# One Mamba-and-experts layer on one core: corrections and u on GpSimd, a PSUM bank for the convolution, three banks for turned states

## The chip, the cores and the metric

The kernel runs on one core of one Trainium2 chip. The metric is device time in microseconds of one execution, the median of three. The core has five engines that take instructions in order, each from its own queue, and wait for each other through semaphores: TensorE (PE), VectorE (DVE), ScalarE (ACT), GpSimd (POOL) and SyncE (SP), which here only issues DMAs. PSUM has eight banks of 128 x 512 float32 values; all eight are in use before and after the change.

## The reference

```python
x = x + mamba(cond(x, subject))          # the part that the change touches
x = x + ffn(adapters(x))                 # experts, after all blocks

# mamba, cut to its shape: 2048 tokens in rows of 64, 1024 channels, 16 states
xz = hidden @ in_proj.T;  x, z = split(xz)
xc = silu(sum(conv_w[:, k] * x_padded[:, k:k + L] for k in range(4)))
dt, B, C = split(xc @ x_proj.T)
delta = softplus(dt @ dt_proj.T + dt_bias)
h = h * exp(delta * A_n) + (delta * xc) * B_n      # a scan over tokens, for each state n
y = sum_n(h_n * C_n);  y = (y + xc * D) * silu(z);  out = y @ out_proj.T
```

The softplus is made from max(v, 0) + log(1 + e) with e = exp(-|v|). A *correction* makes the logarithm exact: w = 1 + e is rounded, and e - (w - 1) is what rounding lost; it is added to ln(w). The product delta * xc is called u.

## The kernel before

The 2048 tokens are four blocks (`j`) of 512. Channels lie on partitions, 8 groups (`d`) of 128 of them, tokens along the free axis, so that most tiles are 128 x 512. A block has 32 steps (`m`): two halves of 16, one for channel groups 0 to 3, one for 4 to 7, and in each half a step per state `n`. In one step, for four channel groups `i`:

- ScalarE makes `da` = exp(delta * A) in one of two PSUM banks (L823);
- GpSimd makes `dbx` = u * B from a broadcast row `b_all` that SP loads (L1077), one buffer for each `i`;
- VectorE scans, h = h * da + dbx (L965);
- TensorE turns the four token tiles `t` of the state into PSUM (`hT`, L623), since the sum over states needs tokens on partitions to scale by C;
- VectorE adds tiles 0 to 2, scaled by C, to `yacc` (L977, L983). Tile 3 is scaled by ScalarE into `stage` (L838) and added by a DMA that GpSimd issues (L1083), except in the last two states of a half.

VectorE's order in a step is: scans 0 and 1, the sums of tiles 0 and 1 of the step before, scans 2 and 3, the sum of tile 2. The products of step m + 1 may start when the scans of step m are done, group by group. The DMA of a step adds what ScalarE scaled two steps before.

Beside this, the pieces of `BESIDE` fill the engines: projections of this block and of the next. Each entry is a step. Names matter here: `x`e is an input projection with its convolution, `z`e a gate projection, `dt`d and `ln`d the softplus of channel group d, `cond`, `rank`, `bc`, `out`, `w`, `xr`, `row` other projections and transposes, `turn` the turning of `yacc`, `gate` the product with silu(z). TensorE does a step's pieces in that step, one before turning the first tiles and the others between tiles. ScalarE does them one step later, and so do VectorE's corrections and convolutions, behind the last sum of the step; VectorE's u and GpSimd's half of `ln` come two steps later, on GpSimd behind the step's DMA issue. In the first half ln4 to ln7 stand at steps 3, 5, 7 and 9, in the second ln0 to ln3 (for the next block) at 23 to 26. The last block has no pieces for a next block: no `x`, no ln0 to ln3. Ahead of the blocks the pieces of `AHEAD` run alone. SP loads `b_all` and the projections' weights in one queue, in which each weight load waits until the projection that held its slot is done.

A correction and u are VectorE's (`correct`, `make_u`); GpSimd adds the correction to the logarithm and the sum to delta (`finish_delta`, L1050 and L1052). The convolution is a product by ScalarE into `xc` (L679) and three sums by VectorE in place, in SBUF (L880).

Of the kernel before, what the change touches and what calls it, by code (L numbers as in the profile page):

```python
# [21 lines left out]
P = 128  # L22
# [54 lines left out]
BANKS = 2  # L77

# [139 lines left out]
def mamba(nc, ctx, arena, ident, logits, parts, x_pad, itok, cond_w, cond_b, rows_d, in_wT, xp_wT, dt_wT, out_wT, chan, ident_d,  # L218
# [60 lines left out]
    hT = [ps(f"hT{t}", [P, HT * P]) for t in range(TB)]  # L279
# [34 lines left out]
    sp_step = sem("sp_step")  # L314
    sp_ready = sem("sp_ready")
# [24 lines left out]
    x2_rows = x2_d[0:TOK].rearrange("(k t p) f -> k t p f", t=TB, p=P)  # L340

    with nc.Block() as block:
# [99 lines left out]
        def _(pe):  # L442
# [170 lines left out]
            def turn_h(j, m, tiles):  # L613

                pe.wait_ge(scan_done, j * SCANS + SCAN0 + HT * (m + 1))
                last = (j, m - 1) if m else (j - 1, STEPS - 1)
                for t in tiles:
                    if last[0] >= 0 and shifted(last[1], t):
                        pe.wait_ge(scaled[t], scaled_by_act(*last))
                    elif last[0] >= 0:  # L620
                        pe.wait_ge(sum_done, sums_by_dve(*last, t))
                    for d in range(HT):
                        mm = nc.tensor.transpose(hT[t][:, d * P:(d + 1) * P], h[:, m % RING, d, t * P:(t + 1) * P],  # L623
                                                 ident[:])
                    mm.then_inc(hT_full, 1)
# [8 lines left out]
            for j in range(NBLK):  # L634
                for m in range(STEPS):
# [12 lines left out]
        def _(act):  # L648
# [18 lines left out]
            def conv_in(section, at, e):  # L667

                act.wait_ge(bank_full, at.full + 1)
                if section == "ahead":  # L670
                    if e >= RING:
                        act.wait_ge(conv_step, (TAPS - 1) * (e - RING + 1))
                else:
                    act.wait_ge(conv_step, at.block * ((TAPS - 1) * DT) + (TAPS - 1) * (e - RING + 1))
                    act.wait_ge(u_ready, (at.block - 1) * DT + e + 1)
                    act.wait_ge(skip_ready, (at.block - 1) * DT + e + 1 + SKIP0)
# [54 lines left out]
            def log1p(section, at, d):  # L731
# [8 lines left out]
                nc.scalar.activation(sp_w[:, s, :], sp_e[:, s, :], ACT.Identity, bias=1.0)  # L740
                nc.scalar.activation(u[:, d, :], sp_e[:, s, :], ACT.Ln, bias=1.0).then_inc(sp_ready, 1)
# [1385 lines left out]
```

## Time and profile before

| | us |
|---|---|
| median of three runs | 2019.96 (2019.82 to 2022.29) |
| the profiled execution, own time | 2020.74 |
| its span | 2018.9 |
| PE, DVE, ACT, POOL busy in the span | 1700.3, 1498.0, 854.7, 1087.3 |
| the four blocks, first scan to last | 121.3 to 1185.7 |

A busy share over the whole span hides the stages: VectorE is full in the blocks, TensorE behind them. Read idle time together with what ended it, and by stretches. Instructions of one engine overlap by some 0.06 us in the profile, so the distance between two starts is what one costs.

### The profile page before, as it was taken

To read this page: it belongs to the slowest core of one execution; us is meant where nothing else is said; L and a number is where in the kernel's file an instruction comes from. 1 tells how busy PE (TensorE), PEld (TensorE's weight loads), DVE (VectorE), ACT (ScalarE), POOL (GpSimd) and SP (SyncE) were. 2 spreads that over 40 slices of the span, in tenths; PEclk is the share of its full clock that TensorE was granted. 3 is DMA by queue.
4 is the path that set the end of the run, shared out by engine and by line. 5 is a ranking of instruction groups with operands and counts; after the bars stand their busy time and mean duration, and the time that the engine had idled before them with its cause. 6 is when DMAs were issued, how large, how long until landed. Compare 5 with 4: busy or idle time off the path is not lost. (4 is left out here: it accounts for less than half of the span.)

```text
span 2018.9 us, 28413 instructions
## 1 busy us (share of the span) xinstructions
PE 1700.3 (84%) x7908; PEld 1265.4 (63%) x7908; DVE 1498.0 (74%) x1925; ACT 854.7 (42%) x1274; POOL 1087.3 (54%) x871
## 2 busy tenths in 40 slices
PE   3856787698888888887867778989989999999998
PEld 2345444464545554446545554877868999999997
DVE  0379989999999999899999960567725566656564
ACT  0456656466576466665575531100002223323232
POOL 0079569677589596597797963000004344334433
PEclk9968878698898798887988879899999999999999
DMA  4223323344335244234343453211215666666664
GB/s 99 68 60 90 89 58 79 84 101 105 94 85 139 76 106 117 66 87 134 84 111 88 116 162 123 72 63 63 85 34 130 168 153 148 154 151 146 168 159 75
DMA packets 146915, 211.45 MB, mean 105 GB/s; under 512 B 24976, under 2 KB 83104, under 8 KB 143584
## 3 DMA queue, kind: packets, MB, share of 16 engines
q1 hardware_dynamic: 109200, 132.52, 20.7%
q0 software_dynamic: 32832, 72.12, 19.4%
q10 hardware_dynamic: 4720, 4.86, 0.9%
q8 instruction: 76, 1.25, 0.3%
q14 instruction: 87, 0.71, 0.1%
HBM read 277.64 MB, written 38.15 MB: 156 GB/s over the span
## 5 line engine op out<-in xcount | busy, mean ns | idle before, releaser
L1077 POOL TENSOR_TENSOR arena_kept<-arena_kept,b_all 128x512 f32<-128x512 f32 x512 | 671.8, 1422 | 196.5 <-DVE arena_kept L965 167.5
L965 DVE TENSOR_TENSOR_SCAN arena_kept<-da,arena_kept 128x512 f32<-128x512 f32 x512 | 596.5, 1203 | 37.6 <-PE hT L623 16.6
L823 ACT ACTIVATE da<-arena_kept,a_neg 128x504 f32<-128x504 f32 x512 | 346.9, 685 | 333.9 <-DVE arena_kept L965 330.3
L623 PE MATMUL hT<-ident_kept,arena_kept 128*128 128x128 f32 x2048 | 326.3, 318 | 172.7 <-DVE arena_kept L965 167.5
L623 PEld LDWEIGHTS hT<-ident_kept,arena_kept 128*128 128x128 f32 x2048 | 286.1, 166 | 265.9 <-DVE arena_kept L965 216.9
L472 PE MATMUL bank<-hid,wt 128*128 128x512 f32 x512 | 258.0, 653 | 22.8 <-ACT arena_kept L679 22.1
L983 DVE SCALAR_TENSOR_TENSOR yacc<-hT,c_now,yacc 128x512 f32<-128x512 f32 x376 | 263.4, 730 | 9.8 <-PE hT L623 8.8
L1981 POOL DMA_INDIRECT out<-y,slots_kept x76 | 132.7, 1745 | 238.4 <-issue 155.4
L472 PEld LDWEIGHTS bank<-hid,wt 128*128 128x128 f32 x512 | 105.0, 215 | 136.2 <-issue 111.8
L1617 POOL DMA_DIRECT2D slots_kept<-lists_kept x1 | 0.6, 569 | 253.1 <-DVE lists_kept L1567 253.1
L880 DVE SCALAR_TENSOR_TENSOR arena_kept<-xpad,ch,arena_kept 128x512 f32<-128x512 f32 x96 | 87.5, 911 | 63.0 <-ACT arena_kept L679 60.7
L1849 ACT ACTIVATE gs<-egp 128x352 f32<-128x352 f32 x73 | 33.8, 463 | 234.9 <-PE eup L1181 234.4
L533 PE MATMUL bank<-skip,wt 128*128 128x512 f32 x256 | 123.0, 629 | 2.5 <-DVE skip L914 2.5
L1976 POOL DMA_INDIRECT xg_kept<-x_scratch,slots_kept x72 | 74.8, 1038 | 78.7 <-ACT y L1888 42.2
L1083 POOL DMA_DIRECT2D yacc<-stage x104 | 97.3, 935 | 34.1 <-DVE arena_kept L965 21.0
L1929 DVE TENSOR_TENSOR a<-gs,eup 128x352 f32<-128x352 f32 x73 | 37.8, 518 | 92.3 <-ACT gs L1849 92.3
L1050 POOL TENSOR_TENSOR arena_kept<-arena_kept 128x512 f32<-128x512 f32 x32 | 48.8, 1524 | 101.6 <-DVE arena_kept L888 101.6
L1179 PE MATMUL egp<-w_up_hi_kept,xT_hi 128*128 x292 | 101.0, 346 | 2.9 <-DVE w_up_lo_kept L1173 2.9
L1455 ACT ACTIVATE sgs<-gp 128x512 f32<-128x512 f32 x24 | 14.4, 598 | 197.0 <-PE gp L1181 197.0
L1169 DVE CAST aT_hi<-aT_ps 128x256 fp32r<-128x256 f32 (+1 forms) x144 | 44.4, 350 | 68.5 <-PE aT_ps L1806 68.5
L1180 PE MATMUL egp<-w_up_lo_kept,xT_hi 128*128 x292 | 94.9, 325 | 0.0
L1181 PE MATMUL egp<-w_up_hi_kept,xT_lo 128*128 x292 | 94.7, 324 | 0.0
(217 smaller groups left out, 3394.4 us busy)
## 6 DMA issues: line engine op xcount, KB each, us to landing
w_up_kept<-in_up_T SPq DMA_DIRECT2D x76, 1408.0 KB, 6.1
w_dn_kept<-in_dn_T SPq DMA_DIRECT2D x76, 768.0 KB, 7.4
b_all<-bt_scratch SPq DMA_DIRECT2D x128, 256.0 KB, 3.6
yacc<-stage POOLq DMA_DIRECT2D x104, 256.0 KB, 4.5
wt<-in_in_T SPq DMA_DIRECT2D x64, 256.0 KB, 3.0
wt<-in_out_T SPq DMA_DIRECT2D x32, 256.0 KB, 3.0
x_in<-in_x_pad ACTq DMA_DIRECT2D x16, 256.0 KB
res<-in_x_pad SPq DMA_DIRECT2D x16, 256.0 KB, 4.5
```

The lines of the kernel that those rows point to most:

```text
L472: mm = nc.tensor.matmul(bank[:], w[:, k, :], hid[:, at.block % RING, k, :], start=(k == 0), stop=(k == KM - 1))
L533: mm = nc.tensor.matmul(bank[:], w[:, d, :], skip[:, part * HT + d, :], start=(part == 0 and d == 0), stop=False)
L623: mm = nc.tensor.transpose(hT[t][:, d * P:(d + 1) * P], h[:, m % RING, d, t * P:(t + 1) * P], ident[:])
L823: nc.scalar.activation(out[:, :, 1:], rows[:, :, 1:], ACT.Exp, scale=a_neg[:, d, n:n + 1]) \
L965: nc.vector.tensor_tensor_scan(h[:, n % RING, i, :], da[i % RING][:], dbx[:, i, :], 0.0, ALU.mult, ALU.add).then_inc(scan_done, 1)
L983: nc.vector.scalar_tensor_tensor(out=yacc[:, t, :], in0=hT[t][:], scalar=scalar, in1=yacc[:, t, :], op0=ALU.mult, op1=ALU.add).then_inc(su ...
L1077: nc.gpsimd.tensor_tensor(dbx[:, i, :], u[:, d, :], b_all[:, m % RING, :], ALU.mult) \
L1083: nc.gpsimd.dma_start(out=yacc[:, t, :], in_=stage[:, SHIFTED.index(t), :], accum_op=ALU.add) \
L1179: nc.tensor.matmul(out, lhs_hi, rhs_hi, start=first, stop=False)
L1180: nc.tensor.matmul(out, lhs_hi, rhs_lo, start=False, stop=False)
L1181: return nc.tensor.matmul(out, lhs_lo, rhs_hi, start=False, stop=last)
L1981: nc.gpsimd.indirect_dma_start(out=out_d, out_offset=bass.IndirectOffsetOnAxis(ap=slots[:, r % LISTS, 0:1], axis=0), in_=y[:, r % YS, :], ...
```

## The change

Four things are edited.

1. In the blocks (not ahead of them) the correction is made by GpSimd: ScalarE also makes w - 1 (an added `ACT.Copy` with bias -1, behind the logarithm), GpSimd subtracts, adds, adds, and then makes u as well. VectorE keeps both ahead of the blocks only.
2. The convolution's product and its first two sums go to a PSUM bank of their own, `conv_sum`; the third sum writes `xc`. The waits until `xc` may be overwritten move from ScalarE to VectorE, and ScalarE waits for the tile before.
3. That bank comes from the turned states: `hT` has three banks, used in a ring over all tiles, instead of one for each of four. A tile waits for the sum of the tile three before it. TensorE now turns three tiles, does the other pieces, and turns the fourth.
4. ln1, ln2 and ln3 and dt1 and dt3 move to later steps: ln0 to ln3 stand at 23, 25, 26 and 28.

```diff
-     ["rank1", "w1"], ["bc0", "gate0", "gate1"], ["dt0", "bc1", "gate2", "gate3"], ["ln0", "dt1", "z4"],
-     ["ct", "ln1", "dt2"], ["ln2", "dt3", "w2"], ["ln3", "z5", "w3"], ["z6", "row0"],
-     ["z7", "row1"], ["row2", "row3", "zsilu1"], ["lg"], []],
+     ["rank1", "w1"], ["bc0", "gate0", "gate1"], ["dt0", "bc1", "gate2", "gate3"], ["ln0", "z4"],
+     ["ct", "dt1"], ["ln1", "dt2", "w2"], ["ln2", "z5", "w3"], ["dt3", "z6", "row0"],
+     ["ln3", "z7", "row1"], ["row2", "row3", "zsilu1"], ["lg"], []],
...
-    hT = [ps(f"hT{t}", [P, HT * P]) for t in range(TB)]
+    hT = [ps(f"hT{s}", [P, HT * P]) for s in range(TURNED)]
+    conv_sum = ps("conv_sum", [P, BLK])
...
+    def turned_in(j, m, t):
+        return hT[(j * SUMS + TB * m + t) % TURNED]
...
-                last = (j, m - 1) if m else (j - 1, STEPS - 1)
                 for t in tiles:
-                    if last[0] >= 0 and shifted(last[1], t):
-                        pe.wait_ge(scaled[t], scaled_by_act(*last))
-                    elif last[0] >= 0:
-                        pe.wait_ge(sum_done, sums_by_dve(*last, t))
+                    at = j * SUMS + TB * m + t - TURNED
+                    if at >= 0:
+                        of, step, tile = at // SUMS, at % SUMS // TB, at % TB
+                        if shifted(step, tile):
+                            pe.wait_ge(scaled[tile], scaled_by_act(of, step))
+                        else:
+                            pe.wait_ge(sum_done, sums_by_dve(of, step, tile))
...
-                    turn_h(j, m, range(0, TB // 2))
+                    turn_h(j, m, range(0, TURNED))
                     for piece in mine[1:]:
                         piece_of("body", j, piece)
-                    turn_h(j, m, range(TB // 2, TB))
+                    turn_h(j, m, range(TURNED, TB))
...
-                nc.scalar.mul(xc[:, e, :], banks[at.bank][:], ch[:, e, W0 + TAPS - 1:W0 + TAPS]).then_inc(act_emptied, 1)
+                if section == "body" or e:
+                    act.wait_ge(conv_step, at.block * ((TAPS - 1) * DT) + (TAPS - 1) * e)
+                nc.scalar.mul(conv_sum[:], banks[at.bank][:], ch[:, e, W0 + TAPS - 1:W0 + TAPS]).then_inc(act_emptied, 1)
...
+                if section == "body":
+                    add.then_inc(sp_added, 1)
+                    act.wait_ge(sp_added, at.block * DT + d + 1 - HT)
+                    nc.scalar.activation(sp_w[:, s, :], sp_w[:, s, :], ACT.Copy, bias=-1.0).then_inc(sp_ready, 1)
...
+                    out = xc[:, e, :].rearrange("p (b l) -> p b l", b=BB) if k == TAPS - 2 else part
                     nc.vector.scalar_tensor_tensor(out=out, in0=xpad[:, e % RING, :, k:k + SEQ],
-                                                   scalar=ch[:, e, W0 + k:W0 + k + 1], in1=out,
+                                                   scalar=ch[:, e, W0 + k:W0 + k + 1], in1=part,
...
+                s = d % RING
+                if section == "body":
+                    pool.wait_ge(sp_ready, at.block * DT + d + 1)
+                    nc.gpsimd.tensor_tensor(sp_w[:, s, :], sp_e[:, s, :], sp_w[:, s, :], ALU.subtract).then_inc(corr_ready, 1)
...
+                if section == "body":
+                    pool.wait_ge(delta_step, at.block * (2 * DT) + 2 * d + 2)
+                    pool.wait_ge(xc_ready, at.block * HALVES + d // HT + 1)
+                    nc.gpsimd.tensor_tensor(u[:, d, :], delta[:, d, :], xc[:, d, :], ALU.mult).then_inc(u_ready, 1)
```

On GpSimd, steps 4 to 6 of a block before the change: four products, the DMA issue, the two operations of a piece `ln`, and products again.

```order
20 L1083 DMA yacc<-stage 128x512
21 L1077 TENSOR_TENSOR arena_kept<-arena_kept,b_all 128x512 x4
22 L1083 DMA yacc<-stage 128x512
23 L1050 TENSOR_TENSOR arena_kept<-arena_kept 128x512
24 L1052 TENSOR_TENSOR arena_kept<-arena_kept 128x512
25 L1077 TENSOR_TENSOR arena_kept<-arena_kept,b_all 128x512 x4
```

The same place after it:

```order
20 L1099 DMA yacc<-stage 128x512
21 L1093 TENSOR_TENSOR arena_kept<-arena_kept,b_all 128x512 x4
22 L1099 DMA yacc<-stage 128x512
23 L1060 TENSOR_TENSOR arena_kept<-arena_kept 128x512
24 L1062 TENSOR_TENSOR arena_kept<-arena_kept 128x512
25 L1064 TENSOR_TENSOR arena_kept<-arena_kept 128x512
26 L1068 TENSOR_TENSOR arena_kept<-arena_kept 128x512
27 L1093 TENSOR_TENSOR arena_kept<-arena_kept,b_all 128x512 x4
```

Two operations have become four: the correction (L1060), the two sums, and u (L1068), all ahead of the next step's products.

On TensorE, at the start of block 1, with bank numbers (L456 is `cond`, L533 `out`, L511 `dt`), before:

```order
191 L456 MATMUL bank0<-w_sel,x_in 128x64 x8
192 L623 MATMUL hT2<-ident_kept,arena_kept 128x128 x4
193 L623 MATMUL hT3<-ident_kept,arena_kept 128x128 x4
194 L533 MATMUL bank1<-skip,wt 128x512 x4
195 L623 MATMUL hT0<-ident_kept,arena_kept 128x128 x4
196 L623 MATMUL hT1<-ident_kept,arena_kept 128x128 x4
197 L511 MATMUL bank0<-rank,w_dt 128x512
198 L623 MATMUL hT2<-ident_kept,arena_kept 128x128 x4
199 L623 MATMUL hT3<-ident_kept,arena_kept 128x128 x4
200 L533 MATMUL bank1<-skip,wt 128x512 x4
```

The same place after it:

```order
192 L462 MATMUL bank0<-w_sel,x_in 128x64 x8
193 L631 MATMUL hT2<-ident_kept,arena_kept 128x128 x4
194 L539 MATMUL bank1<-skip,wt 128x512 x4
195 L631 MATMUL hT0<-ident_kept,arena_kept 128x128 x4
196 L631 MATMUL hT1<-ident_kept,arena_kept 128x128 x4
197 L631 MATMUL hT2<-ident_kept,arena_kept 128x128 x4
198 L517 MATMUL bank0<-rank,w_dt 128x512
199 L631 MATMUL hT0<-ident_kept,arena_kept 128x128 x4
200 L539 MATMUL bank1<-skip,wt 128x512 x4
```

The third tile has moved ahead of the second piece (`dt`), and the fourth, alone behind it, takes the bank (`hT0`) that the step's own first tile was turned into.

On VectorE, the steps around a correction before:

```order
32 L983 SCALAR_TENSOR_TENSOR yacc<-hT,c_now,yacc 128x512
33 L888 SCALAR_TENSOR_TENSOR arena_kept<-arena_kept 128x512
34 L965 SCALAR_TENSOR_TENSOR arena_kept<-da,arena_kept 128x512 x2
35 L983 SCALAR_TENSOR_TENSOR yacc<-hT,c_now,yacc 128x512 x2
36 L965 SCALAR_TENSOR_TENSOR arena_kept<-da,arena_kept 128x512 x2
37 L983 SCALAR_TENSOR_TENSOR yacc<-hT,c_now,yacc 128x512
38 L902 TENSOR_TENSOR arena_kept<-arena_kept 128x512
```

After the change such a pair of steps has neither L888 nor L902 (the order names a scan as SCALAR_TENSOR_TENSOR, L965), only scans and sums follow each other:

```order
40 L980 SCALAR_TENSOR_TENSOR arena_kept<-da,arena_kept 128x512 x2
41 L998 SCALAR_TENSOR_TENSOR yacc<-hT,c_now,yacc 128x512 x2
42 L980 SCALAR_TENSOR_TENSOR arena_kept<-da,arena_kept 128x512 x2
43 L998 SCALAR_TENSOR_TENSOR yacc<-hT,c_now,yacc 128x512
44 L980 SCALAR_TENSOR_TENSOR arena_kept<-da,arena_kept 128x512 x2
```

## Rows read from the trace of the kernel before

**Rows 1.** The page's slices: tenths of VectorE's busy share, 50.5 us each

```profile
DVE  0379989999999999899999960567725566656564
```

**Rows 2.** Windows: length, then busy PE, PEld, DVE, ACT, POOL, behind the blocks

```profile
1185.74:2018.90 833.16, 788.47 (x4148) 682.04 (x4148) 455.49 (x802) 171.85 (x236) 242.29 (x168) 0.96 0.46 118
```

**Rows 3.** Groups by line, VectorE, in the blocks: count, busy, mean ns, idle before

```profile
L965 DVE TENSOR_TENSOR_SCAN arena_kept<-da,arena_kept 128x512 f32<-128x512 f32 x512 | 596.5, 1203 | 37.6 <-PE hT L623 16.6 <-ACT da L823 10.0 <-POOL arena_kept L1077 6.6
...
L888 DVE SCALAR_TENSOR_TENSOR arena_kept<-arena_kept 128x512 f32<-128x512 f32 x28 | 48.5, 1732 | 0.0
L902 DVE TENSOR_TENSOR arena_kept<-arena_kept 128x512 f32<-128x512 f32 x28 | 34.0, 1214 | 0.0
```

**Rows 4.** Timeline of VectorE, a bare step: start, duration, operation, count

```profile
562.41 2.34 DVE L965 TENSOR_TENSOR_SCAN arena_kept<-da,arena_kept 128x512 f32<-128x512 f32 x2 [1.84 <-PE hT L623]
564.66 1.39 DVE L983 SCALAR_TENSOR_TENSOR yacc<-hT,c_now,yacc 128x512 f32<-128x512 f32 x2
...
568.85 2.33 DVE L965 TENSOR_TENSOR_SCAN arena_kept<-da,arena_kept 128x512 f32<-128x512 f32 x2
```

**Rows 5.** Timeline of VectorE, block 1: scan 4 after a wait; a correction

```profile
420.00 2.43 DVE L965 TENSOR_TENSOR_SCAN arena_kept<-da,arena_kept 128x512 f32<-128x512 f32 x2 [1.98 <-POOL arena_kept L1077]
...
604.37 3.27 DVE L888 SCALAR_TENSOR_TENSOR arena_kept<-arena_kept 128x512 f32<-128x512 f32 x1
```

**Rows 6.** Timeline of GpSimd, block 1: products, DMA issue, a piece ln

```profile
569.91 0.88 POOL L1083 DMA_DIRECT2D yacc<-stage  x1 [0.16 <-issue]
...
595.73 5.53 POOL L1077 TENSOR_TENSOR arena_kept<-arena_kept,b_all 128x512 f32<-128x512 f32 x4
...
601.24 5.84 POOL L1077 TENSOR_TENSOR arena_kept<-arena_kept,b_all 128x512 f32<-128x512 f32 x4
...
607.73 1.56 POOL L1050 TENSOR_TENSOR arena_kept<-arena_kept 128x512 f32<-128x512 f32 x1
609.36 1.26 POOL L1052 TENSOR_TENSOR arena_kept<-arena_kept 128x512 f32<-128x512 f32 x1
610.58 5.42 POOL L1077 TENSOR_TENSOR arena_kept<-arena_kept,b_all 128x512 f32<-128x512 f32 x4
```

**Rows 7.** Timeline of VectorE: a convolution in step 12 of block 1

```profile
499.14 3.02 DVE L880 SCALAR_TENSOR_TENSOR arena_kept<-xpad,ch,arena_kept 128x512 f32<-128x512 f32 x3
```

**Rows 8.** Timeline of VectorE: a convolution ahead of the blocks

```profile
58.71 2.33 DVE L880 SCALAR_TENSOR_TENSOR arena_kept<-xpad,ch,arena_kept 128x512 f32<-128x512 f32 x3 [1.02 <-ACT arena_kept L679]
```

**Rows 9.** Windows: steps 4 to 11 of blocks 0, 1, 2 and 3

```profile
145.03:212.33 67.30, 45.24 (x198) 31.31 (x197) 67.16 (x72) 44.31 (x73) 60.46 (x50) 0.80 0.39 91
420.00:492.70 72.70, 63.37 (x282) 39.75 (x282) 71.97 (x70) 44.80 (x73) 62.95 (x52) 0.91 0.46 109
700.19:772.11 71.92, 62.33 (x277) 39.42 (x277) 71.20 (x71) 45.11 (x74) 62.97 (x52) 0.91 0.44 106
980.81:1043.51 62.70, 45.77 (x209) 30.25 (x207) 62.70 (x65) 40.12 (x65) 60.94 (x51) 0.90 0.42 101
```

**Rows 10.** Timeline of VectorE: block 1's last step, first scan of block 2

```profile
656.68 2.34 DVE L965 TENSOR_TENSOR_SCAN arena_kept<-da,arena_kept 128x512 f32<-128x512 f32 x2 [2.35 <-PE hT L623]
...
667.11 1.22 DVE L965 TENSOR_TENSOR_SCAN arena_kept<-da,arena_kept 128x512 f32<-128x512 f32 x1
```

**Rows 11.** Timeline of TensorE, steps 18 and 19 of block 1

```profile
559.98 1.53 PE L623 MATMUL hT<-ident_kept,arena_kept 128*128 128x128 f32 x8 [3.13 <-DVE arena_kept L965]
561.30 4.89 PE L472 MATMUL bank<-hid,wt 128*128 128x512 f32 x8
...
566.90 3.60 PE L483 MATMUL bank<-arena_kept,w_xp 128*128 128x512 f32 x8
```

**Rows 12.** Windows of the same place: busy us of engines, then granted clock

```profile
560.00:564.00 4.00, 4.00 (x12) 2.45 (x13) 2.16 (x3) 3.97 (x7) 1.57 (x3) 0.57 0.02 4
564.00:590.00 26.00, 24.42 (x102) 13.06 (x101) 24.16 (x27) 18.36 (x25) 22.86 (x20) 1.00 0.46 101
```

**Rows 13.** Timeline of GpSimd, the products of step 4 of block 1

```profile
418.61 4.96 POOL L1077 TENSOR_TENSOR arena_kept<-arena_kept,b_all 128x512 f32<-128x512 f32 x4 [5.16 <-DMA b_all<-bt_scratch]
```

More of the change, by code:

```diff
@@ L77 @@
 BANKS = 2
+TURNED = 3
 BODY = [piece for pieces in LINE for piece in pieces]
@@ L314, in mamba @@
     sp_step = sem("sp_step")
+    sp_added = sem("sp_added")
     sp_ready = sem("sp_ready")
@@ L615, in turn_h @@
                 pe.wait_ge(scan_done, j * SCANS + SCAN0 + HT * (m + 1))
-                last = (j, m - 1) if m else (j - 1, STEPS - 1)
                 for t in tiles:
-                    if last[0] >= 0 and shifted(last[1], t):
-                        pe.wait_ge(scaled[t], scaled_by_act(*last))
-                    elif last[0] >= 0:
-                        pe.wait_ge(sum_done, sums_by_dve(*last, t))
+                    at = j * SUMS + TB * m + t - TURNED
[5 more added lines that the diff above has]
+                            pe.wait_ge(sum_done, sums_by_dve(of, step, tile))
                     for d in range(HT):
-                        mm = nc.tensor.transpose(hT[t][:, d * P:(d + 1) * P], h[:, m % RING, d, t * P:(t + 1) * P],
+                        mm = nc.tensor.transpose(turned_in(j, m, t)[:, d * P:(d + 1) * P], h[:, m % RING, d, t * P:(t + 1) * P],
                                                  ident[:])
@@ L669, in conv_in @@
                 act.wait_ge(bank_full, at.full + 1)
[L670 to L673, printed above, removed]
+                if section == "body" or e >= RING:
                     act.wait_ge(conv_step, at.block * ((TAPS - 1) * DT) + (TAPS - 1) * (e - RING + 1))
-                    act.wait_ge(u_ready, (at.block - 1) * DT + e + 1)
-                    act.wait_ge(skip_ready, (at.block - 1) * DT + e + 1 + SKIP0)
                 rows = banks[at.bank][:].rearrange("p (b l) -> p b l", b=BB)
                 nc.scalar.copy(xpad[:, e % RING, :, TAPS - 1:], rows)
-                nc.scalar.mul(xc[:, e, :], banks[at.bank][:], ch[:, e, W0 + TAPS - 1:W0 + TAPS]).then_inc(act_emptied, 1)
+                if section == "body" or e:
+                    act.wait_ge(conv_step, at.block * ((TAPS - 1) * DT) + (TAPS - 1) * e)
+                nc.scalar.mul(conv_sum[:], banks[at.bank][:], ch[:, e, W0 + TAPS - 1:W0 + TAPS]).then_inc(act_emptied, 1)
             def silu_x(at, half):
@@ L872, in _, with conv @@
         def _(dve):
-            def conv(at, e):
+            def conv(section, at, e):
                 dve.wait_ge(act_emptied, at.act + 1)
-                out = xc[:, e, :].rearrange("p (b l) -> p b l", b=BB)
+                if section == "body":
+                    dve.wait_ge(u_ready, (at.block - 1) * DT + e + 1)
+                    dve.wait_ge(skip_ready, (at.block - 1) * DT + e + 1 + SKIP0)
+                part = conv_sum[:].rearrange("p (b l) -> p b l", b=BB)
                 for k in range(TAPS - 1):
@@ L947, in piece_of @@
                 if name == "x":
-                    conv(at, i)
+                    conv(section, at, i)
                 elif name == "ln":
@@ L1026, in _ @@
                         for piece in at_step(j, m - 1):
-                            if name_and_number(piece)[0] in ("x", "ln"):
+                            if name_and_number(piece)[0] == "x":
                                 piece_of("body", j, piece)
-                    if m >= 2:
-                        for piece in at_step(j, m - 2):
-                            if piece.startswith("ln"):
-                                make_u(Place("body", j, piece), name_and_number(piece)[1])
                     if n == NST - 1:
@@ L1035, in _ @@
                             add_state(j, g, n, t)
-                for piece in at_step(j, STEPS - 2):
-                    if piece.startswith("ln"):
-                        make_u(Place("body", j, piece), name_and_number(piece)[1])
             for i in range(HT):
@@ L1063, in piece_of @@
                 if name == "ln":
-                    finish_delta(Place(section, j, piece), i)
+                    finish_delta(section, Place(section, j, piece), i)
                 elif name == "gate":
```

17 lines of the change are left out of this document (10 added, 7 removed).

## The prediction

> **What bounds the kernel now.** The page's slices come first [rows 1]: VectorE stands at nine tenths from the fourth slice to the twenty-third but for two. So the change acts on the four blocks, up to 1186 us; the 833 us behind them, where TensorE is busy for 788 [rows 2], stay as they are. The grouped view of VectorE in the blocks shows what fills it [rows 3]: 512 scans of 1.20 us, and the small groups that the change touches, longer than their work. Idle time before scans is only 37.6 us in all. A bare step takes 6.44 us from scan to scan [rows 4]: two scans, two sums, two scans, one sum. Whatever VectorE does behind the last sum lengthens its step.
>
> Why are the small groups long? One correction takes 3.27 us [rows 5] while GpSimd works through a group of products from 601.24 to 607.08 [rows 6]. A convolution's three sums take 3.02 us beside GpSimd [rows 7] and 2.33 ahead of the blocks, where GpSimd is idle [rows 8]. The difference is a wait for GpSimd's instruction. The scans, which read one of their inputs from PSUM, keep their 1.20 us.
>
> GpSimd is the engine to read next [rows 6]. Its products of one step and the DMA issue behind them take 5.5 us (595.73 to 601.24) against VectorE's 6.44: 0.9 us of room in a step. The two operations of a piece "ln" take 1.63 (607.73 to 609.36, with the wait for the first's end) and 1.22 (to 610.58).
>
> **GpSimd's share after the change.** "ln" now has four operations there, each waiting for the one before: 1.63 + 1.34 + 1.34 + 1.22 = 5.5 us, where 1.34 is a duration of 1.26 and the 0.08 that the first pair shows between an end (609.29) and the next start. A step with "ln" costs GpSimd 11.0 us, it and a bare one 16.6. VectorE without corrections needs 2 x 6.44 = 12.9 for such a pair; with them the pair took 62.7 / 4 = 15.7 in the last block [rows 9]. So where "ln" stands in every second step GpSimd becomes the bound, and of the 82.5 us that leave VectorE (48.5 + 34.0, [rows 3]) little comes back.
>
> *Steps 4 to 11, in which ln4 to ln7 are finished.* Let step 4 start at 0. GpSimd is tied to the scans until its products for step 5 are done; in a bare step that starts at 562.41 [rows 4] the issue behind them is at 569.91 [rows 6], so 7.5 in, and takes 0.6. The first chain runs from 8.1 to 13.6. The first product for step 6 ends at 14.9 and scan 6 starts there, 2.0 later than VectorE could. Two more pairs at 16.6 put step 10 at 48.1. Steps 10 and 11 carry a convolution each: 2 x (6.44 + 2.33) = 17.5, just over GpSimd's 16.6. Step 12 starts at 65.6; in the last block, which has no convolution, at 64.7. The four stretches took 67.3, 72.7, 71.9 and 62.7 us [rows 9]. Gain: 1.7 + 7.1 + 6.3 - 2.0 = **13.1 us**.
>
> *Convolutions in steps 12 to 17.* Of the 18 in three blocks 11 show the 0.7 us (3.02 for 2.33) of [rows 7]. Now the running sum lies in PSUM, one SBUF tensor is read, and the wait should go. Bounds: 0, if TensorE is next in these steps, and 7.6, if all comes back. The row nearest is the scan's, untouched beside GpSimd: I take **6 us**. PSUM in place of SBUF as output isn't in the trace for this operation; sums that read PSUM take 1.39 for two [rows 4], as long as a convolution's two, so 0. The single sum bank makes ScalarE wait for the tile before; ahead of the blocks VectorE idles 1.02 us before each tile [rows 8], longer than ScalarE's operation, so the wait is over when it is asked for: 0.
>
> *Steps 24 to 31 of blocks 0 to 2*, where ln0 to ln3 now stand at steps 23, 25, 26 and 28 and are finished two steps later. In block 1 GpSimd starts the products for step 24 at 595.73 [rows 6] and is behind from there: three bare steps and four with "ln" are 3 x 5.5 + 4 x 11.0 = 60.5; then 1.3 to scan 31 and the 10.4 that the last step takes (656.68 to 667.11, [rows 10]). That ends at 667.9 to 668.5, against 667.11. **Loss: 1.3 us a block, 3.9 in all.** The 2.35 us that scan 31 waited before are covered by it.
>
> *ScalarE* gets 28 more operations. It is idle behind its decays for most of every step (page: 42% busy), and what they feed is GpSimd's chain, which starts a step later. Cost 0; bound 28 x 0.6 = 17.
>
> *TensorE's order.* The fourth turned tile of a step needs the bank of the same step's first, whose sum VectorE ends 3.0 us into the next step (564.66 and half of 1.39, against 562.41, [rows 4]); the projections of the next step stand behind it. Before, four tiles could be turned as soon as the last scan was done. TensorE has 1.8 us of turning and 3.4 to 7.8 us of projections in a step (eight matmuls are 3.60, [rows 11]) and is nearly full where steps are short: 24.4 of 26 us busy from 564 to 590 [rows 12]. A pause costs twice, since the clock falls: from 560 to 564, behind a pause of 3.13 us [rows 11], the granted share is 0.57, so mostly 1.2 GHz, and eight matmuls take 4.89 instead of 3.60. In step 18 of block 1 the projection w0 ran before that pause; with the new order it stands behind a tile that waits for a sum in step 18, and fills the pause instead, and z3 comes 3 us later. Walking on from there, scan 20 is late by 0.6 and the first sum behind it by 1.5: 2 us in blocks 1 and 2. Steps 9 to 15 lose 1.5 and steps 1 to 4 lose 0.5 by the same walk; there SP's queue takes part, since it waits for a projection before it loads the next b_all: GpSimd waited 5.16 us for that load [rows 13] and scan 4 then 1.98 [rows 5]. Block 0, with fewer projections, 1. **Loss: 9 us**; bounds 0, and 32 for 1 us in each of 32 crowded steps.
>
> Sum: -13.1 - 6 + 3.9 + 9 = -6.2 us. The profiled execution took 2020.74 us, 0.8 above the median of 2019.96; the median less 6 is **2014 us**.
>
> The Trainium skill has a rule against such a move: Perfetto Trace Analysis, section Optimizing Scalar/DVE Operations, says that VectorE and GpSimd share an SBUF read port, so that shifting work between them might not help; by it alone, 2020. SBUF — State Buffer, section Who interferes with whom, confines the sharing to VectorE instructions with two SBUF inputs or in a two-port mode. The trace agrees with the second: the scans keep 1.20 us, corrections don't, and few of the latter's kind are left beside GpSimd's new work.
>
> **Rivals.**
> *GpSimd bounds the "ln" stretches, TensorE takes back a part*: as above, 2005 to 2016. 0.45.
> *Gain and loss meet*: TensorE loses 15 instead of 9. 2016 to 2024. 0.2.
> *The late fourth tile decides*: steps 1 to 4 and 9 to 22 of blocks 0 to 2, less those in which ScalarE's silu is waited for, are some 32; 1 us in each makes -15.2 + 32 = +17, 2037. It makes the kernel slower from 0.5 us a step. For it: TensorE all but full [rows 12], and the clock. Against: 3.7 us of room in each second step that GpSimd delays. 0.22.
> *GpSimd's operations cost more*: each of four takes the 1.56 of the one behind a DMA issue: 0.25 x 3 x 28 = 21 more, 2035. Against: the next already takes 1.26 [rows 6]. 0.08.
> *VectorE stays the bound*: the 82.5 us and 8 of the convolutions come back, 1930. It would need the chain hidden; 16.6 against 12.9 forbids that. 0.05.
>
> The range reaches over the first two and the nearer part of the third and fourth: 2000 to 2031. About 0.2%, 4 us, is what a measurement of this kernel can tell from no change. Faster by more: most of the first and the last, 0.5; within: 0.2; slower: 0.3.
>
> **What the next profile would show.** If right: VectorE without corrections or u in the blocks; GpSimd over nine tenths busy in steps 4 to 11 and 24 to 31; scans that wait for GpSimd's products, over 20 us in all, at every second step of 4 to 11; pairs there of 16.6 us; steps 4 to 11 of the last block longer than before. The convolution's three sums at 2.3 to 2.5 us. The TensorE term is wrong if scans and sums outside those stretches wait over 25 us more for turned tiles, or not at all. The whole is wrong if GpSimd's dependent operations take far from 1.3 us, or if no scan waits for GpSimd.

## The result, and the profile after

The changed kernel takes 2047.91 us (median of 4, 2044.63 to 2048.60), the kernel before beside it 2019.89: 1.0133 times as long, 95% interval 1.0115 to 1.015. I had forecast 2014 us with a range of 2000 to 2031. It is 28 us slower, where I expected 6 us less. The profiled execution took 2047.51 us.

The page's slices come first, of VectorE, GpSimd and the granted clock, as [rows 1] for before:

```profile
DVE  0377987888887879877879870376736566655564
POOL 0079769689589697697897955000004444344343
PEclk9966998598898789886877779899999999999999
```

VectorE is no longer at nine tenths. It has lost 82.5 us of corrections and u, and in the blocks it now waits, as the groups of the blocks (line, engine, operation, count, busy us, mean ns, idle us before and releasers) show for VectorE, then TensorE, ScalarE and GpSimd:

```profile
L980 DVE TENSOR_TENSOR_SCAN arena_kept<-da,arena_kept 128x512 f32<-128x512 f32 x512 | 598.9, 1206 | 122.8 <-POOL arena_kept L1093 48.6 <-ACT da L834 33.1 <-PE hT L631 29.8
L998 DVE SCALAR_TENSOR_TENSOR yacc<-hT,c_now,yacc 128x512 f32<-128x512 f32 x371 | 260.8, 733 | 33.1 <-PE hT L631 25.6 <-DMA yacc<-stage 7.0
L895 DVE SCALAR_TENSOR_TENSOR conv_sum<-xpad,ch,conv_sum 128x512 f32<-128x512 f32 x48 | 36.0, 750 | 0.8
...
L631 PE MATMUL hT<-ident_kept,arena_kept 128*128 128x128 f32 x2032 | 335.3, 313 | 205.3 <-DVE yacc L998 104.8 <-DVE arena_kept L980 66.2 <-ACT stage L849 26.3
...
L849 ACT ACTIVATE stage<-hT,c_now 128x512 f32<-128x512 f32 x104 | 70.3, 676 | 42.5 <-DMA yacc<-stage 42.4
...
L1060 POOL TENSOR_TENSOR arena_kept<-arena_kept 128x512 f32<-128x512 f32 x28 | 47.9, 1711 | 0.0
L1062 POOL TENSOR_TENSOR arena_kept<-arena_kept 128x512 f32<-128x512 f32 x28 | 35.6, 1271 | 2.2
```

Idle time before scans went from 37.6 us [rows 3] to 122.8, and all three other engines are among the releasers. The convolution's sums take 0.75 us each: that wait is gone, as forecast. Next the windows (length, busy PE, PEld, DVE, ACT, POOL, granted clock, DMA share, GB/s), steps 4 to 11 of the four blocks as in [rows 9], then steps 24 to 31:

```profile
145.20:212.23 67.03, 49.43 (x203) 32.72 (x203) 56.49 (x64) 45.40 (x77) 64.51 (x55) 0.73 0.38 87
424.10:493.56 69.46, 61.70 (x269) 37.95 (x268) 56.87 (x62) 44.75 (x75) 68.52 (x58) 0.88 0.47 108
709.70:778.00 68.30, 59.00 (x269) 37.21 (x268) 56.66 (x63) 44.93 (x75) 67.36 (x57) 0.90 0.45 106
993.04:1060.50 67.46, 49.47 (x216) 30.34 (x214) 52.39 (x56) 42.87 (x70) 66.52 (x57) 0.86 0.41 94
...
313.74:389.59 75.85, 46.87 (x188) 29.34 (x187) 56.02 (x64) 44.14 (x68) 70.04 (x59) 0.71 0.37 87
599.77:675.55 75.78, 60.26 (x257) 39.18 (x256) 56.22 (x63) 46.90 (x76) 70.10 (x59) 0.78 0.46 122
882.81:958.92 76.11, 59.68 (x257) 39.92 (x256) 56.21 (x63) 46.90 (x76) 70.13 (x59) 0.78 0.45 121
1151.83:1211.60 59.77, 49.60 (x224) 35.06 (x222) 51.75 (x56) 34.63 (x52) 45.87 (x40) 0.83 0.60 164
```

Steps 4 to 11 took 272.3 us in all against 274.6, so 2.4 were won where 13.1 were forecast. The same steps 24 to 31 took 68.21, 69.39, 70.17 and 57.04 us before; the first three stretches lost 20.0 us where 3.9 were forecast. Steps 18 to 23 of all blocks lost 4.9 us, steps 1 to 3 lost 2.8, and steps 12 to 17 won 6.9 in blocks 0 to 2 and lost 4.6 in block 3. GpSimd is busy for 68.52 of 69.46 us in block 1. Its timeline there (start, duration, line, operation, count) is that of an engine with no gap:

```profile
433.07 1.16 POOL L1099 DMA_DIRECT2D yacc<-stage  x1
433.66 1.89 POOL L1060 TENSOR_TENSOR arena_kept<-arena_kept 128x512 f32<-128x512 f32 x1
435.63 1.28 POOL L1062 TENSOR_TENSOR arena_kept<-arena_kept 128x512 f32<-128x512 f32 x1
436.99 1.27 POOL L1064 TENSOR_TENSOR arena_kept<-arena_kept 128x512 f32<-128x512 f32 x1
438.33 1.27 POOL L1068 TENSOR_TENSOR arena_kept<-arena_kept 128x512 f32<-128x512 f32 x1
439.56 5.00 POOL L1093 TENSOR_TENSOR arena_kept<-arena_kept,b_all 128x512 f32<-128x512 f32 x4
444.46 0.86 POOL L1099 DMA_DIRECT2D yacc<-stage  x1
```

From 433.66 to 439.56 the four operations hold the queue for 5.9 us. A whole pair of steps is 16.9.

TensorE's timeline in the same pair shows the ring of three, and the two windows under it its clock:

```profile
427.31 0.77 PE L631 MATMUL hT<-ident_kept,arena_kept 128*128 128x128 f32 x4 [1.37 <-DVE yacc L998]
427.88 5.19 PE L539 MATMUL bank<-skip,wt 128*128 128x512 f32 x8
```

```profile
428.00:431.00 3.00, 3.00 (x5) 1.23 (x5) 3.00 (x4) 1.37 (x2) 3.00 (x4) 0.50 0.85 186
431.00:433.00 2.00, 2.00 (x6) 0.85 (x5) 1.95 (x2) 0.69 (x1) 2.00 (x2) 0.98 0.01 1
```

The fourth tile waits 1.37 us for a sum. Behind the pause the granted clock is 0.50, the level of 1.2 GHz, and the next projection takes 5.19 us instead of 3.60 [rows 11]. So one late tile costs TensorE 1.4 + 1.6 us here.

The last timeline is of step 25 of block 1, and it runs through every engine:

```profile
608.80 0.69 ACT L849 ACTIVATE stage<-hT,c_now 128x512 f32<-128x512 f32 x1 [1.68 <-DMA yacc<-stage]
...
609.54 1.11 PE L631 MATMUL hT<-ident_kept,arena_kept 128*128 128x128 f32 x4 [1.78 <-ACT stage L849]
609.78 0.88 POOL L1099 DMA_DIRECT2D yacc<-stage  x1 [0.67 <-ACT stage L849]
...
610.44 1.92 PE L517 MATMUL bank<-rank,w_dt 128*128 128x512 f32 x2
...
612.40 0.69 ACT L731 ACTIVATE arena_kept<-bank,ch 128x512 f32<-128x512 f32 x1 [2.91 <-PE bank L517]
...
614.07 1.28 ACT L834 ACTIVATE da<-arena_kept,a_neg 128x504 f32<-128x504 f32 x2
...
614.79 1.22 DVE L980 TENSOR_TENSOR_SCAN arena_kept<-da,arena_kept 128x512 f32<-128x512 f32 x1 [4.07 <-ACT da L834]
```

GpSimd had issued its DMA at 602.70, late in its full queue. ScalarE scales the fourth tile only when that DMA has landed; in a ring of three, TensorE's third tile of the next step waits for this scaling; the projection dt1 stands behind that tile, ScalarE's softplus behind dt1, the decays behind the softplus, and the scan behind the decays: 4.07 us.

### The profile page after: what moved, and what is told of

The parts are those of the page before. It is cut to its first block and busy times, and to the rows that moved or that the text cites. A ratio compares the mean times of both kernels' runs of the same rounds, so it can differ in the third digit from the quotient of the medians.

```text
span 2045.7 us, 28442 instructions
## 1 busy us (share of the span) xinstructions
PE 1719.4 (84%) x7908; PEld 1253.5 (61%) x7908; DVE 1409.8 (69%) x1869; ACT 866.1 (42%) x1302; POOL 1147.2 (56%) x927
## 5 line engine op out<-in xcount | busy, mean ns | idle before, releaser
L1093 POOL TENSOR_TENSOR arena_kept<-arena_kept,b_all 128x512 f32<-128x512 f32 x512 | 657.8, 1414 | 161.8 <-DVE arena_kept L980 138.8
L980 DVE TENSOR_TENSOR_SCAN arena_kept<-da,arena_kept 128x512 f32<-128x512 f32 x512 | 598.9, 1206 | 122.8 <-POOL arena_kept L1093 48.6
L631 PE MATMUL hT<-ident_kept,arena_kept 128*128 128x128 f32 x2048 | 338.6, 314 | 207.1 <-DVE yacc L998 104.8
L631 PEld LDWEIGHTS hT<-ident_kept,arena_kept 128*128 128x128 f32 x2048 | 271.5, 161 | 326.4 <-DVE arena_kept L980 216.5
L1997 POOL DMA_INDIRECT out<-y,slots_kept x76 | 136.9, 1802 | 249.5 <-issue 186.0
L478 PE MATMUL bank<-hid,wt 128*128 128x512 f32 x512 | 253.0, 643 | 4.4 <-ACT conv_sum L684 3.4
L539 PE MATMUL bank<-skip,wt 128*128 128x512 f32 x256 | 128.8, 653 | 2.8 <-DVE skip L929 2.8
L1062 POOL TENSOR_TENSOR arena_kept<-arena_kept 128x512 f32<-128x512 f32 x32 | 40.6, 1270 | 104.0 <-DVE arena_kept L903 101.8
L1196 PE MATMUL eup<-w_up_lo_kept,xT_hi 128*128 x292 | 93.6, 321 | 0.0
L1197 PE MATMUL eup<-w_up_hi_kept,xT_lo 128*128 x292 | 93.6, 321 | 0.0
```

The costliest lines, as they stand in the source:

```text
L478: mm = nc.tensor.matmul(bank[:], w[:, k, :], hid[:, at.block % RING, k, :], start=(k == 0), stop=(k == KM - 1))
L539: mm = nc.tensor.matmul(bank[:], w[:, d, :], skip[:, part * HT + d, :], start=(part == 0 and d == 0), stop=False)
L631: mm = nc.tensor.transpose(turned_in(j, m, t)[:, d * P:(d + 1) * P], h[:, m % RING, d, t * P:(t + 1) * P], ident[:])
L980: nc.vector.tensor_tensor_scan(h[:, n % RING, i, :], da[i % RING][:], dbx[:, i, :], 0.0, ALU.mult, ALU.add).then_inc(scan_done, 1)
L1093: nc.gpsimd.tensor_tensor(dbx[:, i, :], u[:, d, :], b_all[:, m % RING, :], ALU.mult) \
L1196: nc.tensor.matmul(out, lhs_hi, rhs_lo, start=False, stop=False)
```

## The experiments

Each is given with its ratio to the kernel before, timed beside it, and the 95% interval. An interval reaches 0.1 to 0.3% to each side, so a difference between two of these runs is uncertain by 3 to 7 us. Sums over steps are read from the starts of the scans in the profiled executions. Runs a to d take the change apart.

**a: the move to GpSimd and the new places alone.** Four banks, turned two and two, convolution in SBUF.

```diff
-TURNED = 3
+TURNED = 4
-                nc.scalar.mul(conv_sum[:], banks[at.bank][:], ...)
+                nc.scalar.mul(xc[:, e, :], banks[at.bank][:], ...)
```

> The changed kernel with the convolution sums back in SBUF and four banks for turned states, turned two, pieces, two: only the move to GpSimd and the moved pieces are left. Theory of the coupling (with a ring of three the third tile of a step waits for ScalarE's scaling of the fourth tile of the step before, which waits for a late DMA; the projections and ScalarE's softplus stand behind, and VectorE waits for decays): that chain is cut, steps 4 to 11 stay at pairs of 16.9 us, steps 24 to 31 lose under 3 us a block, 2018 to 2030 us. Rival, GpSimd's work alone costs it: steps 24 to 31 stay 6 us longer, the convolutions' 7 us are lost again, 2048 to 2056 us.

2057.56 us, 1.0182 (1.0155 to 1.0209). The rival is right: GpSimd's move costs time without any ring. Even the rival's 2048 to 2056 us was just exceeded. Some of the 36 us is the convolution's, as the group of its sums shows, and under it VectorE's timeline in step 10 of block 1:

```profile
L893 DVE SCALAR_TENSOR_TENSOR arena_kept<-xpad,ch,arena_kept 128x512 f32<-128x512 f32 x72 | 83.0, 1153 | 1.7
...
490.04 8.81 DVE L893 SCALAR_TENSOR_TENSOR arena_kept<-xpad,ch,arena_kept 128x512 f32<-128x512 f32 x3
```

The 72 sums took 69.4 us before, and the mean of 1.15 us hides where the rest is: outside step 10 a sum takes 0.75 us or, the first of three, up to 1.6, as before [rows 7]. In step 10 of blocks 1 and 2, where GpSimd goes from products straight into its four operations, the first one takes 5.45 and 5.50 us. These steps take 15.3 us where the changed kernel, with the running sum in PSUM, takes 8.8. What is left for the move itself is run y's to say.

**b and c: ring and convolution without the move.** Both keep VectorE's corrections and the old places, and both turn three tiles, do the pieces, and turn the fourth; c also keeps the convolution in SBUF.

> The kernel before with the ring of three and the convolution sums in PSUM; corrections and u stay on VectorE and the pieces in their old steps. Theory of the coupling: without GpSimd's chain the DMA is issued in time, the ring costs what steps 1 to 3 and 18 to 23 of the changed kernel show, 1 to 3 us a block, the convolutions give 7: 2015 to 2025 us. Rival, the ring alone costs about 1 us in each crowded step: 2035 to 2045 us.

> The kernel before with the ring of three alone, three tiles, pieces, one tile. Whatever the ring costs in run b, this one should be 5 to 7 us above it if the convolution sums in PSUM are worth what the changed kernel's steps 12 to 17 show. Theory of the coupling: 2021 to 2031 us. Rival of the ring alone: over 2040 us. If the gain in steps 12 to 17 came from elsewhere, equal to run b.

b: 2032.15 us, 1.006 (1.0039 to 1.0081). c: 2045.44 us, 1.0119 (1.0091 to 1.0147). The ring, with the order of tiles that belongs to it, costs 24 us, as the rival had it with over 2040, and the convolution in PSUM gives back 13, which puts b between its two expectations. The prediction's 9 us for the ring was too low by more than half. By blocks c is 1.0 us shorter than before in block 0 and 5.6, 5.1 and 13.3 us longer in blocks 1, 2 and 3. VectorE's corrections and u, which nothing moved in c, took 90.5 us instead of 82.5: that is 8 of the 23 us that the blocks lost. In c TensorE's waits before turned tiles name sums for 141.5 us. In the kernel before, 167.5 of 172.7 us named the scans. Of c:

```profile
L629 PE MATMUL hT<-ident_kept,arena_kept 128*128 128x128 f32 x2032 | 330.0, 313 | 204.1 <-DVE yacc L989 133.6 <-DVE arena_kept L971 53.5 <-DVE yacc L983 7.9
```

**d and k: the moved pieces.** d is the changed kernel with the old table, k the kernel before with the new one.

> The changed kernel with the pieces of steps 23 to 28 in their old steps. Theory of the coupling: the pieces' places matter little, within 5 us of the changed kernel, 2043 to 2053 us. Rival, the moved pieces cause the 23 us in steps 24 to 31: 2020 to 2030 us. With four consecutive ln pieces the chains of GpSimd follow step on step, which by 11 us each could also make it slower, up to 2060 us.

> The kernel before with the moved pieces of steps 23 to 28 alone. VectorE's work stays the same and only its steps change: 2016 to 2024 us. If three ln pieces in consecutive steps crowd TensorE and GpSimd before, as they do in the changed kernel (7 us), 2010 to 2016 us.

d: 2054.81 us, 1.0171 (1.0143 to 1.0199), so the new places are worth some 7 us to the changed kernel. In it only two of the four chains on GpSimd still follow step on step, which I take for the reason. k: 2022.86 us, 1.0005 (0.9995 to 1.0014), no difference. The moved pieces aren't the cause.

**e, f and w: two reliefs, alone and together.** e turns two tiles, does the pieces, and turns two; f makes the quantity u on VectorE; w has both.

```diff
-                    turn_h(j, m, range(0, TURNED))
+                    turn_h(j, m, range(0, TB // 2))
...
-                    nc.gpsimd.tensor_tensor(u[:, d, :], delta[:, d, :], xc[:, d, :], ALU.mult).then_inc(u_ready, 1)
```

> The changed kernel with TensorE turning two tiles, then the projections, then two tiles, the ring of three kept. If the projections cost time because they stand behind the third tile, whose bank waits for ScalarE's scaling of the step before's fourth: 2035 to 2043 us, and TensorE's waits for that scaling go from 26 us to under 10. If the late sums are what the ring costs, two late tiles instead of one stand behind projections: 2048 to 2058 us.

> The changed kernel with u, the last of GpSimd's four operations, back on VectorE. If GpSimd's own work bounds a pair of steps (16.9 us, of which 5.9 for the four operations), a pair takes 15.6 us: 1.3 us less in each of 28 ln steps that has no cover elsewhere, some 20 to 32 us in all, 2016 to 2028 us. If the pairs are held by the DMA and ScalarE's scaling or by TensorE, less than 8 us comes: over 2040 us.

> The changed kernel with two tiles, projections, two tiles and with u on VectorE. Alone they gave 11 and 10 us. If they relieve two bounds that hold the same steps, together they give more than the sum, 2012 to 2026 us; if each relieved the same time, 2030 to 2037 us.

e: 2036.67 us, 1.0075 (1.0058 to 1.0092). f: 2038.07, 1.0084 (1.0068 to 1.0101). w: 2021.44, 1.0003 (0.9992 to 1.0014). Against the changed kernel they give 11, 10 and 26 us. That looks like more than the sum, as I had expected of w, but the 5 us between are within the uncertainty, and the blocks of the profiled executions, 4.0, 20.4 and 21.5 us shorter, don't show it. (That of e took 8 us more than its median, that of f 7 us less.) f alone missed its numbers. The pairs of steps 4 to 7 in block 1 stayed at 16.82 and 16.60 us, though GpSimd had only 15.5 us of work in one (16.9 less 1.35), because TensorE, behind the late tile and at the lower clock, and then the load of b_all, came in nearly as late, as GpSimd's row shows for the latter. With both reliefs, in w, they still took 16.68 and 16.72:

```profile
434.59 1.30 POOL L1093 TENSOR_TENSOR arena_kept<-arena_kept,b_all 128x512 f32<-128x512 f32 x1 [1.21 <-DMA b_all<-bt_scratch]
```

**g: u alone on GpSimd, nothing else of the change.**

> The kernel before with u alone on GpSimd; correction on VectorE, convolution in SBUF, four banks, old places. GpSimd's chain is then 4.2 us and an ln pair 15.2, VectorE's 14.5: if the bound is simply the larger of the two, 2008 to 2020 us. Rival: the correction on VectorE waits longer beside a GpSimd that is never idle, and GpSimd's chain waits for the correction: 2022 to 2035 us.

2031.49 us, 1.0048 (1.0031 to 1.0065): the rival came true. One operation of 1.3 us for each of 28 pieces, taken off VectorE and put on the other queue, makes the kernel 10 us slower, and steps 24 to 30 are 12.5 us longer. Not all of it is the queue: the corrections that stay on VectorE now take 2.34 us in the mean, where they took 1.73 [rows 3], 17 us in all, and the scans wait 14 us more for GpSimd's products:

```profile
L888 DVE SCALAR_TENSOR_TENSOR arena_kept<-arena_kept 128x512 f32<-128x512 f32 x28 | 65.4, 2335 | 0.0
```

**n: the ln pieces of the first half spread** over steps 3, 6, 9 and 11.

> The changed kernel with ln5, ln6 and ln7 at steps 6, 9 and 11 in place of 5, 7 and 9, so that two of the four groups of GpSimd's operations fall into steps with a convolution, in which VectorE needs 8.7 us. If GpSimd's queue sets the pairs, the two pairs of 16.9 us in steps 6 to 9 shrink to about 13 and 15: 5 us less in each block, 2026 to 2034 us. If TensorE sets them as well, 2 us a block at most: 2038 to 2045 us.

2055.68 us, 1.0163 (1.0147 to 1.0178), slower than the changed kernel: a miss. Steps 6 and 7 of block 1 have no ln work on GpSimd now, and still take 17.05 us, as the window says; GpSimd's row under it has the wait that took the place:

```profile
440.51:457.56 17.05, 14.31 (x64) 8.82 (x63) 13.15 (x15) 10.34 (x18) 11.59 (x11) 0.90 0.49 111
```

```profile
456.16 2.50 POOL L1093 TENSOR_TENSOR arena_kept<-arena_kept,b_all 128x512 f32<-128x512 f32 x2 [5.04 <-DMA b_all<-bt_scratch]
```

GpSimd waits 5.04 us for b_all. SyncE's queue, which loads it, also waits for projections before it loads weight tiles, and I take this for the reason: in block 0, which has no such projections there, the eight steps did get 2.6 us shorter.

**p, q and s: the fourth tile behind the next step's first projection**, so that nothing stands behind its wait. p is b with this order, q the changed kernel with it, s has spread pieces and u on VectorE as well.

```diff
+                    left = [m - 1] if m and shifted(m - 1, TB - 1) else []
                     for piece in mine[:1]:
                         piece_of("body", j, piece)
+                    for step in left:
+                        turn_h(j, step, range(TURNED, TB))
...
```

> Run b (ring of three and convolution sums in PSUM, no move to GpSimd) with one thing changed in TensorE's order: the fourth tile of a step is turned behind the first projection of the next step, so that nothing stands behind a tile that waits for a sum. If the 23 us of the ring are this wait (with the slower clock that follows it): 2008 to 2018 us, under run b by 15 to 24, and below the kernel before. If the ring costs through ScalarE's scaling or the order of anything else: over 2026 us.

> The changed kernel with the same new place for the fourth tile. If GpSimd alone bounds the ln pairs, they stay at 16.9 us, and only steps outside them get shorter: 2034 to 2042 us. If TensorE behind the late tile was the bound there as well, 2024 to 2034 us. No effect: over 2044 us.

> The changed kernel with all three reliefs: fourth tile behind the next projection, ln pieces of the first half spread, u back on VectorE. If the late tile and GpSimd's queue are the two causes, both are cut: 2000 to 2014 us, below the kernel before. If a third thing holds the steps (ScalarE's decays behind waiting pieces in steps 24 to 31): 2018 to 2028 us.

p: 2060.24 us, 1.018 (1.0157 to 1.0203). q: 2086.12, 1.0327 (1.0313 to 1.0341). s: 2083.61, 1.0283 (1.0257 to 1.0309). All three are far slower, and my cure was wrong. In p TensorE's wait for VectorE's sums falls from b's 121 us to 45, but ScalarE, which scales that tile, now stands 84 us waiting for it with its decays queued behind, and in the ring the third tile of the next step waits for the scaling in turn:

```profile
L846 ACT ACTIVATE stage<-hT,c_now 128x512 f32<-128x512 f32 x104 | 70.6, 678 | 98.0 <-PE hT L630 84.2 <-DMA yacc<-stage 13.8
```

**Runs u and v: weight tiles loaded one step later** (`step_of(piece) + 3` for `+ 2`), run u in the changed kernel, run v in the kernel before.

> The changed kernel with SyncE loading each weight tile one step later, so that it does not wait for a projection ahead of the next b_all. If the late b_all loads are a third bound of the ln pairs and of steps 3 and 7: 2034 to 2043 us, GpSimd's 23 us of waits for b_all under 5. If GpSimd and TensorE bind anyway: 2044 to 2052 us; later tiles could also stop TensorE: over 2052 us.

> The kernel before with SyncE loading each weight tile one step later. GpSimd waited 28.7 us for b_all in the blocks and scans 6.6 us for GpSimd: if the load's place is what cost it, 5 to 10 us less, 2010 to 2017 us. If the waits were covered: 2018 to 2024 us.

Run u (not the quantity): 2049.44 us, 1.0145 (1.0127 to 1.0163), no difference to the changed kernel, though GpSimd's wait for b_all fell from 22.8 to 3.9 us. v: 2014.05, 0.9969 (0.9956 to 0.9982). The load's place is worth 6 us to the kernel before, and nothing to the changed one; whether it would help with the pieces spread as in n, no run shows. v won 13 us in steps 1 to 11 and lost 10 in steps 24 to 30.

**t: the convolution's gain with four banks kept.** x0 to x4 are summed in the bank that their projection filled. TensorE takes that bank again only when the sums are done, and x0 to x4 are projected second in their steps.

```diff
+                    if use.last.summed:
+                        pe.wait_ge(conv_step, use.last.summed)
...
-                out = xc[:, e, :].rearrange("p (b l) -> p b l", b=BB)
+                    part = banks[at.bank][:].rearrange("p (b l) -> p b l", b=BB)
```

> The kernel before with x0 to x4 of blocks 1 to 3 summed in their own projection bank in PSUM, turned states in four banks, and x0 to x4 projected second in their steps. If the convolution's 0.7 us come from the two SBUF operands and TensorE's hold of the bank is covered: 15 times 0.7 less what the bank costs, 2008 to 2018 us. If the longer hold of a bank stops TensorE's projections: 2024 to 2040 us.

2002.87 us, 0.9915 (0.9896 to 0.9934): faster than both kernels, and than the 2008 to 2018 that I expected. The sums took 56.5 us instead of 69.4, which is 13 of the 17. t changes the sums' bank and the order of the projections together; no run has the order alone.

**y: the GpSimd move on top of t.** Four banks, convolution in its projection's bank; only the move and the new places differ from t.

> Run t with corrections and u on GpSimd and the pieces of steps 23 to 28 moved: the whole change, but with four banks and the convolution in its projection bank. If GpSimd's queue is a bound of its own (11.4 us for an ln step, 16.9 for a pair): 10 to 20 us over run t, 2013 to 2023 us. If the move only costs beside the ring of three: 1998 to 2008 us.

2028.90 us, 1.004 (1.0027 to 1.0053), 26 us above t, more than the 10 to 20 that I expected. This is the price of the move by itself, with its new places. Of y, the scans' group in the blocks, and GpSimd in block 1's steps 29 to 31:

```profile
L991 DVE TENSOR_TENSOR_SCAN arena_kept<-da,arena_kept 128x512 f32<-128x512 f32 x512 | 599.5, 1207 | 126.1 <-POOL arena_kept L1104 79.5 <-ACT da L844 23.9 <-PE hT L636 18.9
```

```profile
649.42 1.15 POOL L1110 DMA_DIRECT2D yacc<-stage  x1
650.01 1.86 POOL L1071 TENSOR_TENSOR arena_kept<-arena_kept 128x512 f32<-128x512 f32 x1
651.95 1.27 POOL L1073 TENSOR_TENSOR arena_kept<-arena_kept 128x512 f32<-128x512 f32 x1
653.29 1.27 POOL L1075 TENSOR_TENSOR arena_kept<-arena_kept 128x512 f32<-128x512 f32 x1
654.63 1.27 POOL L1079 TENSOR_TENSOR arena_kept<-arena_kept 128x512 f32<-128x512 f32 x1
655.86 4.95 POOL L1104 TENSOR_TENSOR arena_kept<-arena_kept,b_all 128x512 f32<-128x512 f32 x4
```

The scans idle 126.1 us again, against 34.6 in t, and 79.5 of them are GpSimd's, with no ring of three in the kernel. VectorE has 82.5 us less to do than in t, and the blocks are 27 us longer.

**x: t and the later tiles joined**, the latter for steps 0 to 19 only.

> Run t with weight tiles of steps 0 to 19 loaded one step later (those of steps 20 to 31 as before, since run v lost 10 us in steps 24 to 30 and won 13 in steps 1 to 11). If the two gains are independent: 2003 less 13, 1986 to 1996 us. If run t already took the same time out of steps 4 to 11: 1996 to 2003 us.

1991.67 us, 0.9854 (0.9836 to 0.9872), 11 us under t. The gains add, as far as the intervals tell. It is the fastest version here, and VectorE's slices are full again:

```profile
DVE  0379999999999999999999931757635656656564
```

## Why the prediction was wrong

The signs that I named for the next profile mostly came true: corrections gone from VectorE, GpSimd over nine tenths busy, pairs near 16.6 us, the last block's steps 4 to 11 longer (67.46 for 62.70 us), the convolution at 2.25 us. The mechanism was seen; two terms of the sum were mis-sized, both towards a gain. Against the kernels with four banks the GpSimd terms account for some 21 of the 34 us between forecast and result, and TensorE's order for 10 to 15.

*The GpSimd terms are the step that failed most.* "Steps 4 to 11", a gain of 13.1, and "steps 24 to 31", a loss of 3.9, made -9.2 us together. In the blocks y takes 67.21, 69.19, 68.72 and 68.46 us for steps 4 to 11 and 72.93, 73.99, 73.61 and 56.88 for steps 24 to 31: in all, against before, -1.0 and +12.6. Within it, from the rows:
- In the pairs of steps 4 to 9 the four operations take 5.9 us and not 5.5: the first takes 1.89 us there, where I had taken 1.56 [rows 6]. A pair is 16.9, not 16.6.
- I let GpSimd enter step 4 with the slack of a bare step, its first chain at 8.1 us and scan 6 at 14.9. The window row of block 1 begins at 424.10 and the chain at 433.66, 9.6 us in, since GpSimd had waited for b_all in step 3, which [rows 5, 13] already showed. Scan 6 came at 16.9. That is 2 us in each of blocks 1 to 3.
- In steps 24 to 31 of block 1 the changed kernel's GpSimd takes from 597.79 to 661.96, 64.2 us for what I had put at 60.5. Two groups of products take 7.1 and 7.0 us with their issue instead of 5.5: 3.1 of the 3.7. In the second the issue waits 1.19 us for ScalarE's scaling. In the first it waits 0.67, and the products themselves take 5.82; [rows 6] had this group at 5.84, and at 6.5 with its issue (601.24 to 607.73), where my sum took 5.5. In y the same stretch is 62.4 us. At the end of step 31 VectorE waits 1.8 us for GpSimd's last DMA, which now leaves late.

I had counted that queue's time, but neither what it waits for nor who waits for what it issues.

*"ScalarE", cost 0,* left out a path. I had asked only what its 28 added operations cost, and no run shows them alone. But its decays wait behind pieces that TensorE delivers late: 33.1 us of scans' idle time name it, against 10.0 [rows 3]. In b and c, with the ring and without the move, it is 12.5 and 9.8, in y, without the ring of three, 23.9: most of it comes with the move.

*TensorE's order, a loss of 9*, was 24 us alone (run c) and 19 beside the GpSimd move (the changed kernel over y), inside my bounds of 0 to 32. (The second figure also holds what the two places of the convolution's sum differ by.) My walk had given blocks 0 to 3 a loss of 1, 4, 4 and 0 us; c has -1.0, 5.6, 5.1 and 13.3. The last block, which I had put at nothing without a reason, has over half. The rival "the late fourth tile decides" had this mechanism, with 32 us for it; I gave it 0.22. What I held against it, "3.7 us of room in each second step that GpSimd delays", fell: the ring costs nearly as much beside the move (19) as alone (24), so little of it hid there. The sign that I had named, that this term is wrong if scans and sums outside steps 4 to 11 and 24 to 31 wait no longer for turned tiles, came true as it stands: 13.9 us against 14.0 before. Within these stretches it was 41.5 against 10.9. The sign was poor, since steps 18 to 23 lost 4.9 us all the same.

*The convolution, 6 us*, was for steps 12 to 17 of blocks 0 to 2, and these won 6.9: this term was right. By b against c the whole is 13, with steps 10 and 11, whose share I had counted under steps 4 to 11. The Trainium skill's rule in SBUF — State Buffer, section Who interferes with whom, is borne out by a's sums with two SBUF inputs, up to 5.50 us beside GpSimd, and 0.75 with one in PSUM. The Trainium skill's other rule that I weighed, Perfetto Trace Analysis, section Optimizing Scalar/DVE Operations, came out right that the move might not help, but in the changed kernel not through a port: the scans kept 1.21 us, and it was GpSimd's queue. In g, where the corrections stay on VectorE, they did grow.

One price among the rivals was off as well: each of four operations at 1.56 instead of 1.26 us is 0.30 and not 0.25 more, which makes that rival 25 us and not 21. Only the first of the four took so long (1.71 us in the mean).

Two paths through the runs close the sum. Before to t is -17 us, t to y +26, y to the changed kernel +19: +28. Or before to c +24, c to b -13, b to d +23, d to the changed kernel -7: +27. What stays open: how much of y's 12.6 us in steps 24 to 31 is ScalarE's order and how much GpSimd's queue, since no run moved ScalarE's pieces alone, and whether the 4 us that t gave beyond its sums' 13 are TensorE's new order or noise.

## What to carry to other kernels

Before work is moved to a half-idle engine, count its queue in the crowded steps and follow what it issues there, DMAs included, to whoever waits for them; a share of 54% over the span said nothing here. A PSUM bank taken from a ring must be priced by the projections that stand behind the wait, in every block, and at the lower clock that follows it; a bank that already holds the operand may do instead, as in t. And when several chains end a step nearly together, cutting one may show nothing there: with 1.3 us off GpSimd's pairs (f), with that and the ring's order (w), the pairs of steps 4 to 7 stayed within 0.3 us of what they were.

## What the runs showed of the hardware

The first GpSimd operation behind a DMA issue took 1.71 us in the mean, up to 1.91, where the three behind it took 1.27 each. A pause of TensorE of 1.37 us was followed by a granted clock of 0.50, and eight matmuls took 5.19 us. A sum of VectorE over two SBUF tensors took 0.75 us at its shortest and, in step 10 of blocks 1 and 2 of run a, 5.45 and 5.50 while GpSimd's products and its first operations behind them ran beside it. The same sum with its running part in PSUM kept 0.75 beside GpSimd's products, in the changed kernel, in t and in y.
